# Graph attention on one core: two neighbouring graphs' attention multiplied together in every second slot, projections a slot later, and the last two graphs' scales turned by TensorE

## What is computed

```python
q, k = x @ Wq.T, x @ Wk.T;  v = x @ Wv.T + bv          # 128x384 each
scores = einsum('bqhd,bkhd->bhqk', q, k) * 384**-0.5 + (adj + adj)
scores = where(any(scores != 0, axis=-1), scores, -inf)
p = nan_to_num(softmax(scores))
out = einsum('bhqk,bkhd->bqhd', p, v).reshape(b, n, h) @ Wo.T + bo
return layernorm(x + out)
```

## Time and profile before

| | |
|---|---|
| time, median of 3 runs | 594.82 us (594.63 to 595.19) |
| the profiled execution | 596.39 us, its span 594.6 us |
| TensorE matmul / weight load | 580.4 us (98%) / 511.8 us |
| VectorE, ScalarE, GpSimd | 466.7, 496.8, 473.6 us |
| chain of work that ended last | PE 92%, DVE 3%, ACT 2%, DMA 1%, issue 1% |
| mean granted clock of TensorE | 0.997 |

### The profile page before, as it was taken

The page is one execution under the profiler, slowest core; times in us unless marked ns, Lnnn a source line. Parts: engine busy times, 40 slices in busy tenths (PEclk is TensorE's granted clock), DMA queues, the critical chain, the costliest instruction groups (busy, mean ns, idle before and its releaser), DMA issues.

```text
span 594.6 us, 23592 instructions
## 1 busy us (share of the span) xinstructions
PE 580.4 (98%) x8448; PEld 511.8 (86%) x8448; DVE 466.7 (78%) x2320; ACT 496.8 (84%) x1974; POOL 473.6 (80%) x753
## 2 busy tenths in 40 slices
PE   9999999999999999999999999999999999999895
PEld 5888888888888888888888888888888888888774
DVE  4677787787787787787787787787787787787995
ACT  5798988888888988988888888988988888887982
POOL 0868878878887887878878887887878878866982
PEclk9999999999999999999999999999999999999998
DMA  8411334242143332324242142322324232123231
GB/s 301 168 40 53 111 92 139 60 139 88 56 145 85 115 93 74 116 92 134 65 139 91 52 146 83 115 93 79 112 93 137 62 92 83 54 92 87 77 95 66
DMA packets 34749, 59.62 MB, mean 100 GB/s; under 512 B 10568, under 2 KB 24008, under 8 KB 34632
## 3 DMA queue, kind: packets, MB, share of 16 engines
q1 hardware_dynamic: 34200, 57.53, 30.6%
q10 hardware_dynamic: 432, 0.59, 0.3%
HBM read 44.50 MB, written 13.62 MB: 98 GB/s over the span
## 4 chain that ended last, share of the span: by engine, by line
PE 92%; DVE 3%; ACT 2%; DMA 1%; issue 1%; POOLq 0%; POOL 0%; DVEq 0%; ACTq 0%
PE qk_ps L373 32%; PE scores_ps L467 17%; PE v_ps L409 15%; PE scores_ps L450 8%; PE qk_ps L427 8%; PE scores_ps L396 8%; ACT probs L533 2%; DVE nscores L632 2%; PE scores_ps L478 1%; PE qk_ps L356 1%; DMA scale_t<-scale_mem 1%; PE spare_ps L427 1%; PE v_ps L478 0%; PE qk_ps L478 0%; PE v_ps L427 0%
## 5 line engine op out<-in xcount | busy, mean ns | idle before, releaser
L533 ACT ACTIVATE probs<-nscores,neg_max 128x128 f32<-128x128 f32 x768 | 297.5, 390 | 7.8 <-DVE neg_max L632 2.8
L632 DVE CUSTOM_DVE_ANT_0 nscores<-scores_ps,adj_n 128x128 f32<-128x128 f32 x768 | 167.4, 287 | 28.4 <-PE scores_ps L396 27.6
L306 POOL TENSOR_TENSOR tree<-nscores 128x256 f32<-128x256 f32 x192 | 144.6, 753 | 4.9 <-DVE neg_max L632 4.9
L533 ACT ACTIVATION_READ_ACCUMULATOR probs<-nscores,neg_max 128x1 f32 x768 | 144.9, 189 | 0.0
L558 ACT ACTIVATE probs_t<-qk_ps 128x384 f32<-128x384 f32 (+1 forms) x127 | 62.5, 492 | 69.0 <-PE spare_ps L427 68.9
L467 PE MATMUL scores_ps<-w_o,att_t 128*128 128x384 f32 x576 | 113.1, 341 | 1.5 <-DVE neg_max L632 1.5
L409 PE MATMUL v_ps<-w_v,x_t 128*128 128x384 f32 x567 | 109.5, 338 | 2.5 <-ACT probs_t L558 2.5
L332 POOL TENSOR_TENSOR att_t<-att_n,att_t 128x384 fp32r<-128x384 f32 x61 | 62.3, 1021 | 58.8 <-ACT att_t L563 58.5
L409 PEld LDWEIGHTS v_ps<-w_v,x_t 128*128 128x128 f32 x567 | 100.1, 188 | 8.6 <-ACT probs_t L558 3.3
L373 PE MATMUL qk_ps<-x_t,w_q 128*128 128x512 f32 (+1 forms) x540 | 107.2, 343 | 0.1
L373 PE MATMUL qk_ps<-x_t,w_k 128*128 128x512 f32 (+1 forms) x540 | 107.0, 343 | 0.0
(11 more groups left out here) (76 smaller groups left out, 934.6 us busy)
## 6 DMA issues: line engine op xcount, KB each, us to landing
x_n<-xn SPq DMA_DIRECT2D x32, 384.0 KB, 5.1
scale_t<-scale_mem SPq DMA_DIRECT2D x63, 192.0 KB
out<-out_n SPq DMA_DIRECT2D x31, 384.0 KB, 5.4
x_raw<-xt SPq DMA_DIRECT2D x15, 768.0 KB, 7.2
adj_n<-adj SPq DMA_DIRECT2D x32, 128.0 KB, 4.6
scale_mem<-scale_rows SPq DMA_DIRECT2D x63, 16.0 KB
x_raw<-xt SPq DMA_DIRECT2D x3, 256.0 KB, 5.5
nscores<-wq ACTq DMA_DIRECT2D x3, 192.0 KB, 4.2
```

What stands on the lines that cost most here:

```text
L306: nc.gpsimd.tensor_tensor(tree[:, b % 2, low:high, 0:width], src[:, :, 0:width], src[:, :, width:2 * width], ALU.add).then_inc(tree_step, 1)
L533: last = nc.scalar.activation(probs[:, b % 2, h], nscores[:, b % 2, h], ACT.Exp, bias=neg_max[:, b % 2, h:h + 1], scale=-1.0, accum_out=ro ...
L632: last = nc.vector.tensor_tensor_reduce(out=nscores[:, half, h], in0=scores_ps[j][:, m * P:(m + 1) * P], in1=adj_n[:, b // 2 % 2, half], s ...
```

## The change

- `PAIRED` = 58: graphs 0 to 57 are paired. In an odd slot b TensorE does `attend(b - 1)` and `attend(b)` one after the other, in an even slot none. Their banks are `scores_ps[1]` and `scores_ps[2]`.
- The output projection of a paired graph g, with its split, residual and normalisation, comes in slot g + 2 instead of g + 1. Graph 58 and those behind keep g + 1, so that slot 59 has two of them (57 and 58), and slot 1 has none.
- VectorE normalises two graphs in even slots and none in odd ones.
- `probs_t` gets two buffers, `v_n` and `scale_t` four, `scale_mem` four in DRAM, `stats` and `var_eps` two. Waits follow.
- `score` waits for both normalised graphs in one kind of slot and for `residual` in the other. `x_n` is loaded and biased one slot later, and the store of `out` moves to the odd iteration of SP.
- `direct(b)` holds for graphs 62 and 63: the scale of 62 is turned by TensorE too and doesn't go through DRAM. Behind the loop, `attention_high(61)` and `attention_low(61)` come earlier in their queues.

```diff
+PAIRED = NB - GRP - 2
...
-        v_n = sb("v_n", [P, 2, HID])
+        v_n = sb("v_n", [P, 4, HID])
-        probs_t = sb("probs_t", [P, HEADS + KT, P])
+        probs_t = sb("probs_t", [P, 2, HEADS + KT, P])
-        scale_t = sb("scale_t", [P, 2, HID])
+        scale_t = sb("scale_t", [P, 4, HID])
...
         def direct(b):
-            return b == NB - 1
+            return b >= NB - 2
+        def paired(b):
+            return 0 <= b < PAIRED
+        def attended(b):
+            if paired(b):
+                return (b - 1, b) if b % 2 else ()
+            return (b,) if has(b) else ()
+        def put_out(b):
+            return tuple(g for g in (b - 2, b - 1) if has(g) and b - g == (2 if paired(g) else 1))
         def out_bank(b):
-            return scores_ps[2] if b == NB - 2 else scores_ps[0]
+            return scores_ps[2] if b in (PAIRED, NB - 2) else scores_ps[0]
         def att_bank(b):
+            if paired(b):
+                return scores_ps[1 + b % 2]
             return scores_ps[1] if has(b + 1) else scores_ps[3]
...
@@ sync: loads of x_n and stores
-                    if 1 <= pair < NB // 2 - 1:
-                        sp.wait_ge(y_ready, b - 1)
-                        sp.dma_start(x_n[:, (pair + 1) % 2], xn[pair + 1]).then_inc(xn_in[(pair + 1) % 2], DMA)
-                elif b >= 4:
-                    store(b // 2 - 2)
+                    if pair >= 2:
+                        store(pair - 2)
+                elif 2 < b:
+                    sp.wait_ge(y_ready, b - 2)
+                    sp.dma_start(x_n[:, b // 2 % 2], xn[b // 2]).then_inc(xn_in[b // 2 % 2], DMA)
@@ gpsimd
-                if has(b - 1) and b < NB - 2:
-                    attention_low(b - 1)
-                if has(b - 2):
-                    find_rstd(b - 2)
+                if b < NB - 2:
+                    for done in put_out(b):
+                        attention_low(done)
+                for done in put_out(b - 1):
+                    find_rstd(done)
...
-                if 0 <= b < NB - 2:
+                if 0 < b <= PAIRED:
+                    add_bias(b - 1)
+                if PAIRED <= b < NB - 2:
                     add_bias(b)
@@ tensor: score
+                elif b == 3:
+                    pe.wait_ge(scale_found, 2)
+                elif attended(b - 3):
+                    pe.wait_ge(att_done, attended(b - 3)[-1] + 1)
                 else:
-                    pe.wait_ge(att_done, b - 2)
+                    pe.wait_ge(y_ready, put_out(b - 3)[-1] + 1)
@@ tensor: the slots
-                if has(b - 1):
-                    project_out(b - 1)
-                if has(b):
-                    attend(b)
+                for done in put_out(b):
+                    project_out(done, b)
+                for done in attended(b):
+                    attend(done)
@@ scalar
-                if has(b - 1):
-                    attention_high(b - 1)
+                for done in put_out(b):
+                    attention_high(done)
...
+            attention_high(NB - 3)
             keep_turned_low(NB - 2, 0, 1, 2)
-            attention_high(NB - 3)
             attention_high(NB - 2)
@@ vector
-                if has(b - 1):
-                    normalise(b - 1)
-                if has(b - 2):
-                    moments(b - 2)
+                for done in attended(b - 1):
+                    normalise(done)
+                for done in put_out(b - 1):
+                    moments(done)
...
-                if has(b - 1):
-                    residual(b - 1)
+                for done in put_out(b):
+                    residual(done)
             normalise(NB - 3)
             keep_turned_high(NB - 2)
+            attention_low(NB - 3)
             find_scale(NB - 1)
-            attention_low(NB - 3)
             keep_v(NB - 1)
             normalise(NB - 2)
             keep_turned_high(NB - 1)
+            attention_low(NB - 2)
             moments(NB - 4)
-            attention_low(NB - 2)
```

More of the change, by code:

```diff
@@ L146, in build @@
         rows_out = sem("rows_out")
-        scale_in = [sem(f"scale_in{i}") for i in range(2)]
+        scale_in = [sem(f"scale_in{i}") for i in range(4)]
         scale_ready = sem("scale_ready")
@@ L214, in turned_rows @@
         def turned_rows(b, j):
-            return probs_t[:, 0:columns(b), j * D:(j + 1) * D]
+            return probs_t[:, b % 2, 0:columns(b), j * D:(j + 1) * D]
         def turned_bank(b, j):
@@ L247, in _ @@
                     sp.wait_ge(rows_turned, b + 1)
-                    sp.dma_start(scale_mem[b % 2].rearrange("h (r q) -> r h q", q=D),
+                    sp.dma_start(scale_mem[b % 4].rearrange("h (r q) -> r h q", q=D),
                                  scale_rows[:, b % 2]).then_inc(rows_out, DMA)
                     sp.wait_ge(rows_out, DMA * (b + 1))
-                    wait(sp, att_done, b - 1)
-                    sp.dma_start(scale_t[:, b % 2], scale_mem[b % 2, 0:HEADS].rearrange(
+                    wait(sp, att_done, b - 3)
+                    sp.dma_start(scale_t[:, b % 4], scale_mem[b % 4, 0:HEADS].rearrange(
                         "(j m) q -> j (m q)", j=HPT).unsqueeze(1).to_broadcast([HPT, D, KT * P])).then_inc(
-                            scale_in[b % 2], DMA)
+                            scale_in[b % 4], DMA)
                 if b % 2 == 1:
@@ L414, in turn @@
             def turn(b):
-                if not direct(b):
+                if has(b + 1):
                     pe.wait_ge(v_ready, b + 1)
@@ L441, in attend @@
             def attend(b):
-                pe.wait_ge(turned_high, b + 1 + LOWS - lows(b))
+                if not paired(b) or b % 2 == 0:
+                    pe.wait_ge(turned_high, (b + 2 if paired(b) else b + 1) + LOWS - lows(b))
                 if not projected(b):
@@ L450, in attend, with project_out @@
                         last = nc.tensor.matmul(att_bank(b)[j * D:(j + 1) * D, m * P:(m + 1) * P],
-                                                v_n[:, b % 2, h * D:(h + 1) * D], probs_t[:, h],
+                                                v_n[:, b % 4, h * D:(h + 1) * D], probs_t[:, b % 2, h],
                                                 start=True, stop=True)
                 last.then_inc(pv_done, 1)
-            def project_out(b):
+            def project_out(b, found):
                 pe.wait_ge(att_split, b + 1)
-                if has(b + 3):
-                    pe.wait_ge(biased, KT * (b + 4))
+                if found < NB - 2:
+                    pe.wait_ge(biased, KT * (found + 3))
                 else:
@@ L515, in _ @@
             turn(NB - 1)
-            project_out(NB - 3)
+            project_out(NB - 3, NB - 3 + 1)
             attend(NB - 1)
-            project_out(NB - 2)
-            project_out(NB - 1)
+            project_out(NB - 2, NB - 2 + 1)
+            project_out(NB - 1, NB - 1 + 1)
         @block.scalar
@@ L555, in keep_turned_low @@
                 act.wait_ge(turned, b + 1)
-                wait(act, pv_done, b)
+                wait(act, pv_done, b - 1)
                 for j in banks:
@@ L639, in keep_v @@
                 dve.wait_ge(vproj_done, b + 1)
-                wait(dve, pv_done, b - 1)
-                nc.vector.tensor_tensor(v_n[:, b % 2], value_bank(b)[:, 0:HID], bv_rows[:], ALU.add).then_inc(v_ready, 1)
+                wait(dve, pv_done, b - 3)
+                nc.vector.tensor_tensor(v_n[:, b % 4], value_bank(b)[:, 0:HID], bv_rows[:], ALU.add).then_inc(v_ready, 1)
             def keep_first(b):
@@ L654, in keep_turned_high @@
                 dve.wait_ge(turned, b + 1)
-                wait(dve, pv_done, b)
+                wait(dve, pv_done, b - 1)
                 for j in range(lows(b), HPT):
@@ L697, in normalise @@
                     dve.wait_ge(turned_high, b + 1 + LOWS - lows(b))
-                    scale = probs_t[:, HEADS:].rearrange("p m q -> p (m q)")
+                    scale = probs_t[:, b % 2, HEADS:].rearrange("p m q -> p (m q)")
                 else:
-                    dve.wait_ge(scale_in[b % 2], DMA * (b // 2 + 1))
-                    scale = scale_t[:, b % 2]
+                    dve.wait_ge(scale_in[b % 4], DMA * (b // 4 + 1))
+                    scale = scale_t[:, b % 4]
                 nc.vector.tensor_tensor(att_n[:, b % 2], att_bank(b)[:, 0:HID], scale, ALU.mult).then_inc(att_done, 1)
```

22 lines of the change are left out of this document (11 added, 11 removed).

## The result

| | before | after |
|---|---|---|
| median (6 runs each) | 594.61 us (594.38 to 595.19) | 592.01 us (591.44 to 592.69) |
| ratio | | 0.995, 95% interval 0.9939 to 0.9961 |
| the profiled execution, span | 596.39 us, 594.6 us | 591.78 us, 589.9 us |
| PE busy | 580.4 us | 575.2 us |
| mean granted clock | 0.997 | 0.999 |

The change gains 2.6 us in the median, where 6.0 was forecast and the time lies inside the stated range. The two profiled spans stand 4.7 us apart. Why these two numbers differ is one of the questions of the experiments.

The account below looks back on a forecast made before the run. TensorE was taken to bound slots 2 to 57, with other waits in slot 0, slots 58 to 61 and behind the loops. Terms -4.2 + 0.64 + 0.3 - 2.7 = -6.0 us gave 588.8 us, range 586.8 to 592.3.

Parts of the forecast that it names:

- Part 1: Slots 2 to 57, bound by TensorE: one change of tile fewer in each of 28 pairs, -4.2 us.
- The 0.15: Gain per pair in us: attend's 0.79 on the chain against 0.64 of streaming, taken as a tile-shape change.
- the bound of 0.13: Lower value in us of the gain per pair if nothing waits, 3.6 us over slots 2 to 57.
- The estimate by the latency page: Slots 2 to 57: 28 drains at a matmul's constant 0.166 us, 4.6 us in place of 4.2.
- Part 2: Projection moved by a slot: slot 1 gains attend(0), +0.64, loses project_out(0), -1.58; slot 59 +1.58; sum +0.64 us.
- Part 3: Slot 60: two moments of VectorE in front of bias_and_max on the path, +0.3 us, 0 to 0.7.
- More buffers remove waits: Waits in the new order: grown buffers add none, cost 0, covered by TensorE's 8.8 us a slot.
- Part 4: Behind the loops: graph 62's scale without DRAM, clock staying at 2.4 GHz, -2.7 us, bounds -1.4 to -3.6.
- the median of the runs is 0.2 over that span: Last step of the sum: profiled span forecast at 588.6 us, hence a median of 588.8 us.
- A wait that eats a gain: Slots 2 to 57: ScalarE's queue or the wait before turn takes 0.15 us of 28 pairs; 593.0 us, chance 0.10.
- the second rival: Behind the loops: VectorE bounds the end and the clock falls anyway, gain 0 to 1.4; 590.1 to 591.5 us, chance 0.14.
- a tile change that isn't saved: Slots 2 to 57: the pairs gain 0 instead of 4.2 us; 593.0 us, chance 0.10.

Follow-up runs that it names:

- the two experiments: Kernel before with attend(b) ahead of project_out(b - 1), normalise(b) moved, a score wait added: 611.88 us; kernel before with attend(b) cut in two around project_out(b - 1): 616.73 us.
- the four buffers: Changed kernel with four buffers for y and the moments instead of two, residual waiting for the normalisation four graphs before: 591.31 us, ratio 0.9931.
- the last scale alone: Kernel before with only graph 62's scale also turned by TensorE, pairing and lag unchanged, one VectorE wait added: 594.03 us, ratio 0.9976.
- the three profiles: Kernel before, profiled twice (spans 594.6 and 594.4 us), and changed kernel with graph 62's scale through DRAM again (594.94 us, ratio 0.9989).
- the two runs: Changed kernel with four y and moments buffers, GpSimd's add_bias held behind attention_low(61): for graphs 62 and 63, 591.24 us; for 61 to 63, 590.99 us.

## Why the prediction was right in its direction and half wrong in its size

- **Part 1, -4.2 us.** The mechanism held, with no wait on TensorE. Its size was 0.13 to 0.135 a pair: 49.15 to 546.78 in the old timeline and chain against 47.68 to 541.62 in the new, 497.63 less 493.94 is 3.7 us. The 0.15 was a difference of two numbers of two digits; the bound of 0.13 was stated. That from the full array to 32-row tiles costs what 32-column to 32-row tiles do was taken from starts, and bears out. Other changes of tile cost otherwise, as the two experiments show, but the sum didn't need them. The rule of the Trainium skill ("TensorEngine Tiling (Array Packing)", Key Properties) that a change of mode drains the engine fits the trace: the records within a block of tiles stream without a gap, and each block costs 0.14 us more. The estimate by the latency page, 0.166 us a drain, was further off than the row.
- **Part 2, +0.64.** Slot 1: `project` to `project` 40.21 to 49.15 before, 39.67 to 47.68 after, -0.93, as forecast (0.64 - 1.58). Slot 59: +1.60, as forecast.
- **Part 3, +0.3.** Slot 60 had +0.39. Here the failing step stands: I walked through the waits of the regular slots and not through those of the slots where the lag changes. "More buffers remove waits" was said of the buffers that grew; `y` didn't grow, and its wait for `out_ready` two graphs back, which the diff doesn't touch, became late. It cost slot 61 1.45 us, shown by the four buffers.
- **Part 4, -2.7.** In the profiles -2.96, of which `attend(63)` and the clock behaved as written. The step that failed carried it to the median: "the median of the runs is 0.2 over that span". It sets a time beside the span of another execution. In every execution the time is 1.8 us over its span (1.9 to 2.0 in the changed kernel); the profiled 596.39 was 1.8 us slower than the median of 594.6, and its half clock was the reason to suspect. The half clock won back 1.15 us only where it had been there, and not all executions had it. At full clock on both sides the end shrinks from 17.95 to 16.52 us, by 1.43, and in the medians the last scale alone is worth 1.2 to 1.4 us.

The sum, from -6.0: +0.5 for the size of part 1, +1.5 for the missed wait, +0.1 for slot 60 and -0.3 for the end as profiled give -4.2, which is what the two profiles show from slot 1 on. From there to the -2.6 of the medians it is +1.6 for the unusual execution: 1.15 for the half clock, and 0.45 that no run assigns (the longer wait for the DMA, 6.31 against 5.97 us, may be a part). In the spans there is another -0.6: the first exponential started at 22.11 and at 21.53 us. Over all profiles it lies between 21.06 and 22.45, in kernels whose start is the same, so that this is no effect of the change.

Of the rivals, none took place as written. A wait that eats a gain did come, at another place. The end did give little in the median, the -1.4 that the second rival had as its bound, but because the profiled execution had more to win than the median one, and not for VectorE or a clock that fell. That the time lies inside the range at all owes something to luck: the range's upper end was set for a tile change that isn't saved or an end that gives little, not for a missed wait and a wrong base.

## What to carry to other kernels

Where a change alters a lag, list each buffer's wait in the slots where the old lag meets the new one, the untouched ones first: the regular slots had margins and kept them, and the one step between lags cost 1.5 of the 4.6 us that the pairs and slot 1 had won. Before a sum is built on a profiled execution, compare its own time with the median in the same quantity; if they differ, find what in it is unusual, and don't count on winning it. The mean clock of an execution is not enough for that, as it doesn't say where the clock fell. A saved change of tile shape is real, but small enough (0.13 us) that it needs dozens of repetitions on the bounding engine.

## What the hardware showed

- A change of tile on TensorE has three costs here: 0.14 us for a block of tiles of 32 columns, 0.10 us at the end of a block of the full array before tiles, and 0.11 us at the start of one behind 32-column tiles, whose weight loads then start with the matmuls and not 0.12 us ahead.
- Waits of 2.16, 2.03 and 2.38 us were followed by some 3.4 us at half clock in the three profiles that have them, which cost 1.15 us. It isn't so in every execution: 28 of 39 on one chip had no such stretch. 1.9 us of useless matmuls in its place made the kernel faster by 0.16% (0.04 to 0.27).
- A VectorE instruction with both inputs in SBUF took 1.38 us instead of 0.55 when GpSimd's began 0.05 us ahead of it, and 0.55 when none ran. The Trainium skill says so in "SBUF — State Buffer", section Who interferes with whom, and the two runs agree.
